# Long attention: the row maxima turned by one 64-row product in the last round of scores instead of a 128-row product between rounds

## What is computed

```
scores = q @ k.T                       # 896 x 1500 for each of 16 batches
m      = max(scores, axis=-1)          # one maximum for each of 896 rows
p      = exp(scores - m)
out    = (p @ v) / sum(p)
```

## Time and profile before

| what | value |
| --- | --- |
| median of 3 runs | 2386.94 us |
| profiled execution, time | 2381.28 us |
| its span | 2379.5 us |
| TensorE (PE) busy | 2193.1 us, 92% |
| VectorE (DVE) busy | 1475.1 us, 62% |
| GpSimd (POOL) busy | 1093.6 us, 46% |
| ScalarE (ACT) busy | 951.0 us, 40% |
| mean granted TensorE clock | 0.937 |

### The profile page before, as it was taken

One profiled execution on the slowest core, in us unless ns is written; L12 is line 12 of the kernel. 1 busy time (PEld: TensorE's weight loads), 2 busy tenths in 40 slices (PEclk: granted clock), 3 DMA queues, 4 the chain that ended last, 5 costly groups with the idle time before them and its releaser, 6 DMA issues. The chain is left out here.

```text
span 2379.5 us, 37636 instructions
## 1 busy us (share of the span) xinstructions
PE 2193.1 (92%) x13328; PEld 1525.1 (64%) x13328; DVE 1475.1 (62%) x2468; ACT 951.0 (40%) x1433; POOL 1093.6 (46%) x612
## 2 busy tenths in 40 slices
PE   6768998989999998897999999899799999998998
PEld 4447997745555557664555555698365555567997
DVE  2765445277777756787777775412777777745444
ACT  1443443335455451212445455111345445434443
POOL 0331332037777770363777777011067777732332
PEclk9878999779999998997999999879799999998999
DMA  4473632265464513124545542286755544403432
GB/s 82 132 257 88 217 115 65 88 169 124 101 138 106 130 38 124 43 91 114 123 109 117 130 105 60 63 295 266 200 118 118 123 112 110 104 9 102 121 116 81
DMA packets 123971, 285.55 MB, mean 120 GB/s; under 512 B 33371, under 2 KB 76207, under 8 KB 119900
## 3 DMA queue, kind: packets, MB, share of 16 engines
q1 hardware_dynamic: 123164, 281.96, 44.4%
q0 software_dynamic: 672, 1.84, 0.2%
HBM read 237.15 MB, written 46.41 MB: 119 GB/s over the span
## 5 line engine op out<-in xcount | busy, mean ns | idle before, releaser
L1235 DVE TENSOR_REDUCE keep_top<-banks 128x1 f32<-128x500 f32 x945 | 603.7, 674 | 247.4 <-PE banks L1151 242.4
L1305 ACT ACTIVATE att_ex<-banks 125x896 f32<-125x896 f32 x576 | 524.7, 919 | 240.7 <-PE banks L1144 220.3
L1176 PE MATMUL banks<-att_ex,att_v 125*64 125x448 f32 x2304 | 464.7, 545 | 0.0
L1358 POOL TENSOR_TENSOR att_acc<-att_acc,att_ex 125x896 f32<-125x896 f32 x186 | 391.7, 2106 | 73.6 <-ACT att_ex L1305 60.3
L1151 PE MATMUL banks<-keep_kh,keep_qt 64*128 64x500 f32 x1008 | 359.9, 445 | 26.1 <-PEq L574 9.6
L1358 POOL TENSOR_TENSOR att_acc<-att_acc,att_two 125x896 f32<-125x896 f32 x141 | 297.1, 2107 | 161.8 <-DVE att_two L1247 161.8
L1176 PEld LDWEIGHTS banks<-att_ex,att_v 125*64 125x64 f32 x2304 | 152.5, 136 | 246.9 <-issue 187.2
L1144 PE MATMUL banks<-att_sh,att_on 64*125 64x448 f32 x1152 | 297.5, 366 | 0.0
L1144 PE MATMUL banks<-att_ql,keep_kh 64*125 64x448 f32 x1152 | 296.8, 364 | 0.0
L1673 PE MATMUL banks<-moe_xs,moe_w 128*128 128x448 f32 x1272 | 279.7, 370 | 3.9 <-DVE moe_w L1769 2.3
L1247 DVE TENSOR_TENSOR att_two<-att_ex 125x896 f32<-125x896 f32 x144 | 243.0, 1687 | 59.8 <-ACT att_ex L1305 57.3
(11 more groups left out here) (273 smaller groups left out, 2691.6 us busy)
## 6 DMA issues: line engine op xcount, KB each, us to landing
keep_kh<-kvt_hi SPq DMA_DIRECT2D x96, 375.0 KB, 5.2
att_kl<-kvt_lo SPq DMA_DIRECT2D x96, 375.0 KB, 7.2
q_rows<-mats_q SPq DMA_DIRECT2D x24, 896.0 KB, 4.4
keep_qt<-q_rows SPq DMA_DIRECT2D x96, 224.0 KB, 5.8
moe_raw<-L_experts_dram SPq DMA_DIRECT2D x53, 384.0 KB, 4.1
att_v<-kvn SPq DMA_DIRECT2D x24, 720.0 KB
sort_wu<-L_experts_dram SPq DMA_DIRECT2D x14, 1024.0 KB, 10.3
moe_cb<-comb_rows SPq DMA_DIRECT2D x62, 224.0 KB
```

Source lines behind the costliest of these rows:

```text
L1176: last = pe.matmul(PS[WEIGHED][64 * e:64 * e + 64, 0:HALF], v[:, s // 2, u, s % 2, :], ex[:, u % RING, e, :], start=u == 0, stop=u == UNIT ...
L1235: dve.tensor_reduce(top[:, s % 2, n // NS, n % NS:n % NS + 1], PS[6 + (PIECES * s + n) % 2][:, 0:SB], AX.X, ALU.max).then_inc(mx_done, 1)
L1305: act.activation(ex[:, u % RING], scored, ACT.Exp).then_inc(exp_done, 1)
L1358: pool.tensor_tensor(a, a if n else ex[:, 0], two[:, i] if k == 2 else ex[:, k], ALU.add).then_inc(gathered, 1)
```

## The change

`turn` becomes one product of the type float32r: the maxima `nm` (now 64 partitions x 128 columns, of which 14 columns are used and the rest are zero) are the stationary operand and a 64 x 64 identity `eye` the moving one. For this VectorE writes the maxima of partitions 0 to 63 and of 64 to 127 side by side, with two reductions in place of one. The turned maxima are 14 rows of 64, ScalarE copies 14 x 64, and the four DMAs take 4 or 3 rows of 64. `turn` goes from the end of round 1 to place 4 of round 2, and `high` from the end of round 1 to behind the third exponential of round 2. GpSimd clears `nm` and makes `eye` at the start of each stage, ahead of its other preparations, and TensorE and VectorE get a wait on `ones` for it. For batch 0, VectorE now writes the maxima to `top` first and reduces that to `nm` in two more reductions.

```diff
                 def shifts(b):
...
-                    for e, at, tiles, a, z in ((0, 0, (0, 3), 0, 128), (0, 384, (3, 4), 0, 64),
-                                               (1, 0, (3, 4), 64, 128), (1, 64, (4, NT), 0, 128)):
-                        n = (tiles[1] - tiles[0]) * (z - a)
-                        sp.dma_start(sh[64 * e:64 * e + 1, s, at:at + n].rearrange("o (t p) -> o t p", p=z - a).bitcast(FP32),
-                                     nmh[tiles[0]:tiles[1], s, a:z].bitcast(FP32)).then_inc(m_in[s], 16)
+                    for e, odd, t, side in ((0, 0, 0, 0), (0, 1, 0, 1), (1, 0, 3, 1), (1, 1, 4, 0)):
+                        n, row = 4 - odd, side * NT + t
+                        sp.dma_start(sh[64 * e:64 * e + 1, s, :].rearrange("o (g j) -> o g j", j=64)[:, odd::2, :].bitcast(FP32),
+                                     nmh[row:row + n, s, :].bitcast(FP32)).then_inc(m_in[s], 16)
...
                 def turn(s, b):
-                    pe.wait_ge(nm_ready, b + 1)
+                    pe.wait_ge(nm_ready, 2 * b + 2)
                     if not known(b, 2):
                         pe.wait_ge(sm_done, b - 1)
-                    pe.matmul(PS[SUMMED][0:NT, 0:128], nm[:, s % 2, :], G["ident"][:, :],
+                    pe.matmul(PS[SUMMED][:, 0:64], nm[:, s % 2, :], G["eye"][:, :],
                               start=True, stop=True).then_inc(nt_ready, 1)
...
+                            if i == 2 and place == 4 and left:
+                                turn((s + 1) % 4, b + 1)
                             if place < 16:
                                 score(s, b, 4 * i + place // 4, place % 4, half)
...
-                        if i == 1 and left:
-                            turn((s + 1) % 4, b + 1)
-
+
+                pe.wait_ge(ones, 2)
                 pe.wait_ge(qk_in[0], 64 + (l - 1) * B // 4 * 64)
                 for t in range(NT):
...
                 def shift(s, b):
                     dve.wait_ge(mx_done, PIECES * b + PIECES)
-                    dve.tensor_reduce(nm[:, s % 2, :], top[:, s % 2], AX.X, ALU.max, negate=True).then_inc(nm_ready, 1)
+                    if not known(b, 2):
+                        dve.wait_ge(nt_ready, b - 1)
+                    for side in range(2):
+                        dve.tensor_reduce(nm[:, s % 2, NT * side:NT * side + NT], top[64 * side:64 * side + 64, s % 2],
+                                          AX.X, ALU.max, negate=True).then_inc(nm_ready, 1)
...
-                    dve.tensor_reduce(nm[:, 0, t:t + 1], scored, AX.XY, ALU.max, negate=True).then_inc(mx_done, NS)
+                    dve.tensor_reduce(top[:, 0, t, 0:1], scored, AX.XY, ALU.max).then_inc(mx_done, NS)
                 dve.wait_ge(mx_done, PIECES)
-                dve.engine_nop().then_inc(nm_ready, 1)
+                dve.wait_ge(ones, 2)
+                for side in range(2):
+                    dve.tensor_reduce(nm[:, 0, NT * side:NT * side + NT], top[64 * side:64 * side + 64, 0, :, 0:1],
+                                      AX.X, ALU.max, negate=True).then_inc(nm_ready, 1)
...
-                    act.activation(nmh[:, s % 2, :], PS[SUMMED][0:NT, 0:128],
+                    act.activation(nmh[:, s % 2, :], PS[SUMMED][0:2 * NT, 0:64],
                                    ACT.Copy).then_inc(high_done, 1)
...
                             exps(b, u)
+                            if u == 4 * i + 2 and i == 2 and left:
+                                high((s + 1) % 4, b + 1)
...
-                        if i == 1 and left:
-                            high((s + 1) % 4, b + 1)
...
                 pool.wait_ge(G["q_out"][1], HALF_STORES * l)
+                pool.memset(nm[:, :, :].bitcast(FP32), 0.0).then_inc(ones, 1)
+                pool.tensor_copy(G["eye"][:, :], G["ident"][0:64, 0:64]).then_inc(ones, 1)
                 pool.memset(sh[:, :, :].bitcast(FP32), 0.0).then_inc(ones, 1)
```

More of the change, by code:

```diff
@@ L994, in attend_long @@
     with Stage(nc, f"att{l}") as st:
-        kh, q, top, nm, nmh = (G[n] for n in ("kh", "qt", "top", "nm", "nmh"))
+        kh, q, top = (G[n] for n in ("kh", "qt", "top"))
+        nm, nmh = st.sb("nm", [64, 2, 128], F32R), st.sb("nmh", [2 * NT, 2, 64], F32R)
         kl = st.sb("kl", [128, 2, L], F32R)
@@ L1106, in _ @@
                 load_values(0)
-                sp.wait_ge(ones, 1)
+                sp.wait_ge(ones, 3)
                 shifts(0)
@@ L1223, in _ @@
                     top_scores(1, 1, n, n % 2)
-                pe.wait_ge(ones, 3)
+                pe.wait_ge(ones, 5)
                 emit(pe, batch)
@@ L1366, in place @@
                     pool.tensor_tensor(ctxT[:, :, b * S:b * S + S], c, r, ALU.mult).then_inc(placed, 1)
-                pool.wait_ge(ones, 3)
+                pool.wait_ge(ones, 5)
                 for b in range(B):
@@ L2332, in attention @@
             G["kh"], G["qt"] = keep.sb("kh", [128, 4, L], F32R), keep.sb("qt", [128, 4, NH * S], F32R)
-            G["top"], G["nm"] = keep.sb("top", [128, 2, NT, NS]), keep.sb("nm", [128, 2, NT])
-            G["nmh"] = keep.sb("nmh", [NT, 2, 128], F32R)
+            G["top"] = keep.sb("top", [128, 2, NT, NS])
+            G["eye"] = keep.sb("eye", [64, 64], F32R)
         with Stage(nc, f"mats{l}") as st:
```

## The result

The changed kernel takes 2393.4 us in the median of 13 runs (2387.81 to 2398.28), the kernel before 2386.65 us in 13 runs beside it. The ratio is 1.0032, 95% interval 1.0023 to 1.0041: about 7 us slower, clear of noise but a third of the 19 us that were forecast, and close to rival B's time. It lies inside the stated range of 2391 to 2424 us, near its lower edge. Two executions among all runs, one of the kernel before and one of experiment 6, took 5313 and 7852 us and count in no ratio.

What follows compares the result with a forecast made beforehand. TensorE was taken as the bound, busy 34.62 of 35.00 us in long attention. 18.3 + 0.3 - 14.0 + 5.9 + 10.8 = +21.3 us gives 2402.6 on the profiled 2381.3, 2408.2 on the median; forecast 2406, range 2391 to 2424.

Steps and rivals of the forecast that it cites:

- rival B: DMAs before part 3: rows land in time, no wait, inserted turn 0.05 to 0.15 us; +7 to +12, some 2396 us; chance 0.26.
- The wait at the stage's start: TensorE's first piece of each of three stages waits for GpSimd's memset of nm and copy to eye: +18.3 us.
- The turn removed: End of round 1: the turn's 0.31 us between value products and pieces goes, in 45 batches: -14.0 us.
- inserted: Round 2, before unit 10's scores: the turn among the scores costs 0.13 us in 45 batches: +5.9 us.
- Batch 0's turn: Stage start: VectorE adds two reductions ahead of the turn, which saves part of its two passes: +0.3 us in all.
- The moved copy and the DMAs: Round 2 to next batch's part 3: rows land late, TensorE waits 0.24 us in 45 batches: +10.8 us.
- the lack is only 0.2 us: Sign for the rows landing in time: their lateness before part 3 is small, on a price from stores to HBM.
- SyncE's later loads and scales: SyncE's queue behind the four DMAs: scales and loads for the batch after next go out later, counted as nothing.
- The fixed cost of 2.0 us: The four layout DMAs: at the page's price per DMA, an estimated wait of 0.52 us a batch, 23 us in all.

Runs made afterwards that it cites:

- experiment 6: The changed kernel with turn and copy put back to the end of round 1, the wait at the stage's start kept: 2391.46 us, ratio 1.0026.
- experiment 2: The kernel before plus one TensorE wait, for GpSimd's memset of sh, ahead of batch 0's pieces at each stage start: 2408.56 us, ratio 1.0107.
- experiment 8: The changed kernel with the wait moved to batch 0's turn and the turn's product issued twice for all batches but the first: 2384.68 us, ratio 1.0002.

## Why the prediction was wrong

The direction was right and the size was not: +19 us forecast, +7 measured. By its own steps:

- **The wait at the stage's start**, 18.3 us. Right: the pauses grew by 17.6 us, moving the wait behind the pieces brings 16 us back, and with the wait alone a kernel that is otherwise the same gets slower by the 19.7 us of its pauses and some more.
- **The turn removed**, -14.0 us, and **inserted**, +5.9 us at 0.13 each. Right: 0.31 us fell away and 0.11 came in, net 9 us instead of 8.1. Doubling the product confirms the price.
- **Batch 0's turn**, +0.3 us. Too small to be seen in the times. In the traces the first score follows the first piece after 19.64 to 19.66 us instead of 19.57 to 19.61, some 0.2 us over the three stages.
- **The moved copy and the DMAs**, +10.8 us. This is the step that failed. It said that the rows land "0.17 to 0.30 us late", and they land 0.04 us early. The landing had the right price, 1.68 us, and the whole chain from the first issue takes 3.77 us against 3.69 to 3.82. The room before their use was taken as 3.52 us and is 3.81. I had put the copy's 0.27 us behind the end of the exponential and 0.02 for the issue; the copy overlaps the exponential's record and is shorter, 0.19 us, so the first issue comes 0.11 us after that end. And from that end to the load of part 3 there are now 3.92 us, not 3.81: by the rows the inserted turn moves unit 11 and all behind it back by its 0.11 us, and unit 10's exponential not, which gives the DMAs that time too; I had left that out. Both errors have the same sign, and their 0.29 us turn a wait of 0.24 us in each of 45 batches into none. That takes 10.8 us off the sum of +21.3 and leaves +10.5, against +8.6 by the trace; the other terms make up the rest, each within 1 us.
- **The range and the rivals.** Rival B, with a chance of 0.26, described what happened, but only half for its reason. That the lack was small ("the lack is only 0.2 us") was so; the doubt that it raised, a price taken from stores to HBM, was not what failed. A term that is a difference of two sums of 3.5 us and more, each known to 0.1 to 0.2, had no business being the middle of the forecast at full size: half of it, some 5 us, would have been a fairer middle.
- **SyncE's later loads and scales**, nothing. Right: no wait on the keys of the batch after next appeared at round 2.
- **The fixed cost of 2.0 us** that the Trainium skill gives (DMA: Bandwidth & Descriptors, "Anatomy of one DMA") for the path of GpSimd's queue would have put the rows 0.3 us late even in the true room, at an estimated 2.09 + 2.0 = 4.09 against 3.81. Here a small DMA between two places of SBUF lands 1.68 us after its issue begins, and the measurement decides.

## What to carry to other kernels

A wait belongs directly ahead of the first instruction that needs it. Put at the head of a list it also holds back everything that doesn't need it; here one line cost 16 us, more than the whole rewrite of the turn won. When a copy or product is moved later, add up the chain behind it to its last user with all overlaps, in both directions; if the room comes out within 0.3 us of the chain, forecast the two cases, not a mean. And when a change has a new form and a new place, test each alone: the form gave the whole gain, and the place used up all but 0.04 us of the DMAs' slack for nothing. The slack had been some 4 us, 8.1 us from issue to use less the 3.77 us of the chain.

## What was not expected of the hardware

Two instructions of ScalarE overlap in the records: the 14 x 64 copy begins 0.11 us before the exponential ahead of it is recorded as ended (658.40 against 658.51).

The end of the program, behind all long attention, lasted 261.6 us in the trace of the kernel before and 262.0 in that of the changed one, and between 261.5 and 263.9 in those of nine experiments. In experiments 2 and 8 it lasted 267.3 and 267.2, with the same number of products. In the 180 us of experiment 2 shown above TensorE is slower by 2% at the same granted clock of 1.00; experiment 8 has 872 products in the like stretch. Nothing in the code of that part differs, and the cause is not known. A measurement of such a kernel has to leave room for 5 us that come from there.
